# A decoder layer on one core: the expert weights' split moved from GpSimd to ScalarE and VectorE, and the causal mask moved from a matrix product to a GpSimd selection

## The chip, the cores and the metric

The kernel runs on one core of a Trainium2 chip. The metric is the device time of one execution in microseconds. A core has five engines with a queue of instructions each: TensorE (PE in the profile, its weight loads PEld), VectorE (DVE), ScalarE (ACT), GpSimd (POOL) and SyncE (SP), which here only issues DMAs. Every queue runs in order, and the queues wait for each other with semaphores.

## The reference, cut to what matters

```
x (16, 128, 256), ctx (16, 128, 64): 16 sequences of 128 tokens
1. self-attention, 16 heads of 16, one shared key and value head, causal:
     scores = where(key <= query, q k / 4, min);  weights = softmax(scores);  x = layernorm(x + out(weights v))
2. cross-attention on ctx, 32 query heads on 8 key heads of 8, no mask:  x = layernorm(x + xattn(x, ctx))
3. feed-forward: a base network (256 -> 2*512 -> 256, silu(gate)*up) for every token, and 8 experts of the
   same shape of which a token takes the best 2 of softmax(x @ gate_w):
     x = layernorm(x + base(x) + sum over the 2 of share * expert(x))
```

## The kernel before, in words

The work is two blocks one after the other.

**The attention block** is a software pipeline over the 16 sequences. Five lists, `PE_ORDER`, `ACT_ORDER`, `DVE_ORDER`, `POOL_ORDER` and `SP_ORDER`, give each engine its order of stages within one step; an entry is (stage, unit, delta), and in step s the stage works on sequence s + delta. The order is written out by hand, and every stage waits on semaphores for what it reads and for the buffer that it overwrites. `s_` stages belong to self-attention, `c_` stages to cross-attention, `x2_turn` turns the finished row block `stream` over for the second block. Fp32 operands of the big products are split in two (a high part in fp32r and the low remainder), and products are summed from three of the four combinations.

Stages that matter here: `s_max` makes masked scores with queries on the partitions, whose row maxima VectorE takes (L626, a reduction); the maxima go back into the operands (`s_shift`), and `s_main` makes the scores a second time with keys on the partitions. In `s_main` each 512-column bank starts with a bf16 product of the identity with the mask `mask_kq` (L845) and then adds the scores (L846). `s_exp` (ScalarE, L493) takes the exponential into `prob`, `s_sum` (PE, L857) multiplies it with the values, with a column of ones for the denominators. For the layer norms VectorE runs a small chain `newton` of one-column operations (L711, L714, L717) and then `s_ln` (L729) or `c_ln` (L771), which scale a 128x256 tile; in `DVE_ORDER` both L717 and then L729 stand ahead of the maxima of `s_max`.

Beside this, the block splits the experts' weights. For each of 16 halves of expert weights (`HALF` = 1536 columns), SP loads `raw_w` (L359), GpSimd copies the high part (`w_high`, L401) and subtracts for the low part in three pieces (`w_low`, L406), and SP stores both parts to DRAM (`store_w`, L363). Other GpSimd stages are `s_split` (L390, low part of x), `c_keys` (L435, two products), `x_bias` (L426) and, twice in all, `base_split` (L415, L417).

**The experts block** starts behind a barrier. PE computes the router's logits for all tokens (L1432, 32 products that the profile counts as 64), VectorE and ScalarE turn them into choices, the positions of the chosen tokens are found, and 39 sorted tiles of 128 tokens run through the chosen experts while the base network fills in before and after. GpSimd gathers the rows of tile j + 3 (L1107) and scatters the results of tile j (L1113), both as indirect DMAs. The split weights of an expert come back in one 3 MB load (L1067) into one of three slots; the layout in DRAM is `(EXPERTS, P, 2, 2, HALF)`, one piece of 24 KB for each partition. For a sorted tile, PE reads two registers out of SBUF and waits for the weights with one of them:

```
slot_of[j] = pe.value_load(tile_slot[0:1, j:j + 1], min_val=0, max_val=RING - 1)
needed = pe.value_load(tile_ready[0:1, j:j + 1], min_val=1, max_val=EXPERTS)
free_inner(u, h)
if h == 0:
    pe.wait_ge(sem["weights_ready"], needed)
```

Of the kernel before, what the change touches and what calls it, by code (L numbers as in the profile page):

```python
# [7 lines left out]
F32 = mybir.dt.float32  # L8
# [10 lines left out]
P = 128  # L19
# [6 lines left out]
CONST_COLS = 3 * P + 22  # L26
# [13 lines left out]
HT_RING = 5  # L40
ROUTE_COLS = 2 * P + SLOTS + EXPERTS * EXPERTS + PICKS + 1 + EXPERTS
# [16 lines left out]
    ("x2_turn", 0, -2),  # L58
# [13 lines left out]
    ("c_ln", 0, -2), ("c_rows", 0, 1), ("c_den", 0, -1), ("c_den", 1, -1), ("c_out", 0, -1), ("c_out", 1, -1),  # L72
    ("s_max", 1, 3), ("c_res", 0, -1), ("s_den", 0, 2), ("c_stats", 0, -1), ("s_out", 0, 2), ("c_max", 0, 1), ("s_bias", 0, 4),
# [3 lines left out]
    ("s_split", 0, 4), ("w_high", 0, 2), ("c_keys", 0, 1), ("w_low", 0, 2), ("w_low", 1, 2),  # L77
    ("x_bias", 0, 2), ("w_low", 2, 2), ("base_split", 0, 2),
# [3 lines left out]
    ("store_w", 0, 1), ("load_w", 0, 3), ("store_x2", 0, -2),  # L82
# [24 lines left out]
    "x2_turn": [("x2_read", 1, 1)],  # L107
}
# [81 lines left out]
def decoder_layer(nc, x, xT, ctx, ctxT, wqkvT, bqkv, woT, bo, gate_w, base_gu, base_down, expert_w, consts, routing, out):  # L190
    x2 = nc.dram_tensor("x2", (B * S, D), F32, kind="Internal").ap()
    shared = nc.dram_tensor("chosen_y", (CHOICES * B * S, D), F32, kind="Internal").ap()
    split = nc.dram_tensor("split_w", (EXPERTS, P, 2, 2, HALF), F32, kind="Internal").ap()
    with ExitStack() as both:
        def sb(name, shape, dt=F32, scope=both):
# [10 lines left out]
        gate = sb("gate", [P, 2, EXPERTS])  # L206
        base_loaded = both.enter_context(nc.semaphore("base_loaded"))
# [4 lines left out]
                  gate_w, gate, base_hi, base_lo, base_dn, base_loaded, base_split, expert_w, split, split_stored, xT2, x2, x2_stored)  # L212
        experts(nc, split, split_stored, routing, x2, x2_stored, shared, stream, xT2, ident, eps, gate, base_hi, base_lo, base_dn,
# [3 lines left out]
def attention(nc, x, xT, ctx, ctxT, wqkvT, bqkv, woT, bo, consts, stream, ident, eps, base_gu, base_down,  # L217
              gate_w, gate, base_hi, base_lo, base_dn, base_loaded, base_split, expert_w, split, split_stored, xT2, x2, x2_stored):
    score_ring, prob_ring, sum_ring, misc_ring = rings()
    with ExitStack() as scope:  # L220
# [3 lines left out]
        def two(name, shape, dt=F32):  # L224
# [10 lines left out]
        mask_qk, mask_kq = sb("mask_qk", [P, 4, P], BF16), sb("mask_kq", [P, 4, P], BF16)  # L235
        blk_s, blk_c = cst[:, 3 * P:3 * P + 2], cst[:, 3 * P + 2:3 * P + 6]
        neg_s, neg_c = cst[0:32, 3 * P + 6:3 * P + 14], cst[0:32, 3 * P + 14:3 * P + 22]
# [46 lines left out]
        names = """w_high w_low x2_turned x2_read base_high consts_loaded weights_loaded w_hi w_split wo_split tables values_set  # L284
            xT_hi_set xT_split x_biased s_qkv_full s_qkv_read s_rows_hi s_rows_lo s_q_full s_q_read s_k_full s_k_read
            s_max_full s_max_read s_shift_full s_shift_read s_main_full s_exp s_summed s_sum_read
            s_out_full s_den_set s_ctx s_ctx_full s_ctx_hi s_ctx_read s_res_full s_res_read s_stats s_mv s_ln s_rsqrt0
# [33 lines left out]
        def _(sp):  # L321
# [49 lines left out]
            for p in range(2):  # L371
                sp.wait_ge(split_stored[p], 16 * EXPERTS)

        @block.gpsimd
        def _(pool):

            for p in range(2):
                pool.memset(v_s[p][:], 0.0)
                zero = pool.memset(v_c[p][:], 0.0)
# [15 lines left out]
            def w_high(seq, unit):  # L395

                p = seq.odd
                wait_loaded(pool, w_loaded, seq)
                if seq.off >= 2:
                    wait_loaded(pool, split_stored, seq.back(2))  # L400
                pool.tensor_copy(halves[p][:, 0, :], raw_w[p][:]).then_inc(sem["w_high"], 1)  # L401

# [547 lines left out]
def experts(nc, split, split_stored, routing, x2, x2_stored, shared, stream, xT2, ident, eps, gate, base_hi, base_lo, base_dn,  # L950
            base_loaded, base_split, out):
    with ExitStack() as scope:
# [147 lines left out]
        def _(pool):  # L1100
# [16 lines left out]
            for j in range(AHEAD):  # L1117
                gather(j)
# [539 lines left out]
```

## Time and profile before

| what | value |
|---|---|
| median of 3 runs | 762.73 us (762.64 to 770.33) |
| the profiled execution's own time | 764.03 us |
| its span | 762.2 us |
| PE busy | 632.4 us, 83% |
| DVE busy | 476.9 us, 63% |
| ACT busy | 307.3 us, 40% |
| POOL busy | 224.8 us, 29% |

The profile is of one execution. Busy time is a sum over both blocks: the attention block ends at about 411 us, the sorted tiles run from 473 to 704 us, and the rest is the base network and the last layer norm. An engine counts as busy also while its instruction is held up inside.

### The profile page before, as it was taken

The page shows a single profiled execution, that of the slowest core. Times are in us where ns is not written, and L with a number is a line of the kernel's source. Part 1 is how long each engine was busy: PE and PEld are TensorE (multiplying, and loading weights), DVE is VectorE, ACT ScalarE, POOL GpSimd, SP SyncE. Part 2 cuts the span into 40 slices and gives each one's busy share as a digit, 9 for nine tenths or more (in the row PEclk, how much of TensorE's full clock was granted, in tenths as well). Part 3 has the DMA queues.
Part 4 walks back from the last instruction along what each step waited for, and adds up shares of the span by engine and source line. Part 5 has one row for each costly group of instructions (what it writes and reads, how often), then busy time and mean ns, then how long its engine had stood idle before and what let it go on. Part 6 is the DMA issues. An engine that isn't in the chain of part 4 may idle for free. (4 is left out here: it accounts for less than half of the span.)

```text
span 762.2 us, 11308 instructions
## 1 busy us (share of the span) xinstructions
PE 632.4 (83%) x3379; PEld 436.6 (57%) x3379; DVE 476.9 (63%) x972; ACT 307.3 (40%) x657; POOL 224.8 (29%) x223
## 2 busy tenths in 40 slices
PE   3767989898898898899767998997898888998981
PEld 2444435555454545454335876776686776777770
DVE  4578998988888988978762472333333333344286
ACT  2435656655656655565553211222222222223114
POOL 2344653244432244423200002233333333332100
PEclk9989999999999999999997799999999999999997
DMA  8241344413444313342204800015515542110513
GB/s 265 84 152 59 138 138 153 150 65 105 152 139 153 130 65 124 138 145 105 90 14 149 374 0 28 29 53 197 210 42 201 208 152 92 44 47 24 183 39 110
DMA packets 34727, 90.46 MB, mean 119 GB/s; under 512 B 6028, under 2 KB 24975, under 8 KB 33648
## 3 DMA queue, kind: packets, MB, share of 16 engines
q1 hardware_dynamic: 30928, 80.43, 29.5%
q0 software_dynamic: 3744, 9.31, 3.8%
q8 instruction: 32, 0.52, 0.3%
q14 instruction: 23, 0.19, 0.1%
HBM read 56.18 MB, written 34.47 MB: 119 GB/s over the span
## 5 line engine op out<-in xcount | busy, mean ns | idle before, releaser
L1135 ACT ACTIVATE silu<-inner 128x512 f32<-128x512 f32 x55 | 32.9, 598 | 185.4 <-PE inner L1523 135.1
L493 ACT ACTIVATE prob<-scores 128x1024 f32<-128x1024 f32 x96 | 98.2, 1025 | 13.1 <-PE scores L846 7.8
L1296 DVE TENSOR_TENSOR hT<-hiddenT,hT 128x512 fp32r<-128x512 f32 x39 | 27.0, 692 | 111.5 <-ACT hT L1141 111.5
L1113 POOL DMA_INDIRECT chosen_y<-y_rows,to_row x39 | 40.0, 1026 | 161.2 <-DVE y_rows L1311 161.2
L1518 PE MATMUL inner<-weights,sT_hi 128*128 x156 | 69.1, 443 | 20.9 <-issue 20.9
L626 DVE TENSOR_REDUCE max_c<-scores 128x8 f32<-128x1024 f32 x64 | 77.9, 1217 | 5.8 <-PE scores L909 4.3
L919 PE MATMUL scores<-q_c,k_c 128*128 128x512 f32 x128 | 48.0, 458 | 33.3 <-DVE max_s L626 26.9
L390 POOL TENSOR_TENSOR xT_lo<-xT_in,xT_hi 128x256 fp32r<-128x256 f32 x16 | 11.9, 747 | 192.5 <-ACT xT_hi L464 192.5
L1107 POOL DMA_INDIRECT rows<-x,from_row x39 | 38.1, 978 | 91.9 <-DVE from_row L1278 80.4
L933 PE MATMUL sums<-prob,v_c 128*32 128x512 f32 x256 | 63.0, 604 | 0.0
L1519 PE MATMUL inner<-weights,sT_hi 128*128 x156 | 61.8, 396 | 0.0
L406 POOL TENSOR_TENSOR halves<-raw_w,halves 128x512 fp32r<-128x512 f32 x48 | 60.9, 1283 | 0.1
L919 PEld LDWEIGHTS scores<-q_c,k_c 128*128 128x128 f32 x128 | 20.4, 201 | 60.2 <-issue 54.3
L1523 PE MATMUL inner<-weights,sT_lo 128*128 x156 | 49.0, 395 | 0.0
L909 PE MATMUL scores<-k_c,q_c 96*128 96x512 f32 x128 | 45.7, 438 | 3.9 <-DVE max_c L626 3.9
L626 DVE TENSOR_REDUCE max_s<-scores 128x8 f32<-128x1024 f32 x32 | 38.9, 1217 | 14.7 <-PE scores L822 14.6
L1518 PEld LDWEIGHTS inner<-weights,sT_hi 128*128 128x128 f32 x156 | 29.6, 190 | 31.1 <-issue 28.1
L435 POOL TENSOR_TENSOR k_c<-k_split,cst 96x512 fp32r<-96x512 f32 x32 | 32.7, 1043 | 38.8 <-DVE k_split L735 38.8
L1553 PE MATMUL y<-weights,hT 128*128 x156 | 42.7, 305 | 0.5 <-ACT hT L1141 0.4
L822 PE MATMUL scores<-k_s,q_s 96*128 96x256 f32 x128 | 39.8, 427 | 0.0
L1554 PE MATMUL y<-weights,hT 128*128 x156 | 39.7, 286 | 0.0
L857 PE MATMUL sums<-prob,v_s 128*64 128x512 f32 x128 | 34.5, 618 | 0.0
(217 smaller groups left out, 1482.1 us busy)
## 6 DMA issues: line engine op xcount, KB each, us to landing
split_w<-halves SPq DMA_DIRECT2D x16, 1536.0 KB, 6.6
weights<-split_w SPq DMA_DIRECT2D x8, 3072.0 KB, 11.2
raw_w<-in_expert_w SPq DMA_DIRECT2D x16, 768.0 KB, 8.1
weights<-chosen_y SPq DMA_DIRECT2D x8, 512.0 KB, 7.4
xT_in<-in_xT SPq DMA_DIRECT2D x16, 128.0 KB, 2.7
x_in<-in_x SPq DMA_DIRECT2D x16, 128.0 KB, 2.4
x<-stream SPq DMA_DIRECT2D x16, 128.0 KB, 1.7
ctxT_in<-in_ctxT SPq DMA_DIRECT2D x16, 96.0 KB, 2.3
```

The costliest lines, as they stand in the source:

```text
L406: pool.tensor_tensor(halves[p][:, 1, n * third:n * third + n], raw_w[p][:, n * third:n * third + n], f32(halves[p][:, 0, n * third:n * thi ...
L493: act.activation(prob[:, m, :], scores[:, n, :], ACT.Exp, scale=scale).then_inc(sem[exped], 1)
L626: dve.tensor_reduce(out_[:, 8 * unit:8 * unit + 8], scores[:, n, :].rearrange("p (h k) -> p h k", k=S), AX.X, ALU.max).then_inc(sem[read], 1)
L822: mm = pe.matmul(scores[:, n, at + 256 * v:at + 256 * v + 256], q_s[p][0:96, 4 * unit + 2 * bank + v, :], k_s[p][0:96], start=False, stop= ...
L909: mm = pe.matmul(scores[:, n, 512 * v:512 * v + 512], q_c[p][0:96, 2 * unit + v, :], k_c[p][0:96, unit // 2], start=True, stop=True)
L919: mm = pe.matmul(scores[:, n, 512 * v:512 * v + 512], k_c[p][:, a, 2 * (unit % 2) + v, :], q_c[p][:, 4 * a:4 * a + 4, :], start=True, stop ...
L933: mm = pe.matmul(sums[32 * j:32 * j + 32, n, :], v_c[p][:, a, 32 * j:32 * j + 32], prob[:, m, 512 * v:512 * v + 512], start=True, stop=True)
L1113: pool.indirect_dma_start(out=shared, out_offset=bass.IndirectOffsetOnAxis(ap=to_row[:, j:j + 1], axis=0), in_=y_rows[j % 3][:], in_offset ...
L1518: pe.matmul(into, sT_hi[j % 2][:, k, :], w(0, k), start=(k == 0), stop=False)
L1519: pe.matmul(into, sT_hi[j % 2][:, k, :], w(1, k), start=False, stop=False)
L1523: mm = pe.matmul(into, sT_lo[j % 2][:, k, :], w(0, k), start=False, stop=(k == 1))
L1553: pe.matmul(into, hT[:, j % 2, 0, P * c:P * c + P], w(0, c), start=(c == 0), stop=False)
```

## The change

- `mask_kq` and its product in `s_main` go. Between `s_exp` and `s_sum` stands a new GpSimd stage `s_causal`, which sets the weights of later keys to zero in place, by index; `s_sum` waits for it in place of `s_exp`.
- `w_high` moves to ScalarE, in two halves of 768 columns; `w_low` moves to VectorE, in three pieces of 512 columns, one step later. `store_w` comes one step earlier relative to its input. `base_split` comes two steps earlier.
- The split weights lie in DRAM in pieces of 512 columns (2 KB); a half's high and low part are stored by two DMAs, and the load of an expert moves 12 pieces for each partition.
- The logits are computed in the attention block, sequence by sequence (`x2_logit` on PE, then ScalarE copies them to SBUF). The experts block starts without those products.
- The wait for an expert's weights moves from PE to GpSimd: a new `go(j)` reads `tile_ready`, waits and increments a semaphore `go` on which PE waits with a constant. PE keeps the other register.
- An expert's padded count is at least 128; `y_rows` shares memory with `lane_hot`.

```diff
-CONST_COLS = 3 * P + 22
+CONST_COLS = 2 * P + 22
+PIECE = 512
+PIECES = HALF // PIECE
 PE_ORDER = [
...
-    ("x2_turn", 0, -2),
+    ("x2_logit", 0, -3), ("x2_turn", 0, -2),
 ]
 ACT_ORDER = [
...
-    ("s_rsqrt", 0, 1), ("c_read", 1, -1), ("c_rows", 0, 1), ("c_exp", 0, 0), ("s_read", 0, 2),
-    ("c_exp", 1, 0), ("c_turn", 0, 1), ("c_exp", 2, 0), ("c_values", 0, 1), ("s_read", 1, 2),
-    ("c_exp", 3, 0), ("s_rows", 0, 4), ("x2_read", 0, -2),
+    ("s_rsqrt", 0, 1), ("w_high", 0, 2), ("c_read", 1, -1), ("c_rows", 0, 1), ("c_exp", 0, 0), ("s_read", 0, 2),
+    ("c_exp", 1, 0), ("c_turn", 0, 1), ("c_exp", 2, 0), ("c_values", 0, 1), ("w_high", 1, 2), ("s_read", 1, 2),
+    ("c_exp", 3, 0), ("s_rows", 0, 4), ("x2_logit", 0, -3), ("x2_read", 0, -2),
 ]
 DVE_ORDER = [
...
-    ("c_ln", 0, -2), ("c_rows", 0, 1), ("c_den", 0, -1), ("c_den", 1, -1), ("c_out", 0, -1), ("c_out", 1, -1),
-    ("s_max", 1, 3), ("c_res", 0, -1), ("s_den", 0, 2), ("c_stats", 0, -1), ("s_out", 0, 2), ("c_max", 0, 1), ("s_bias", 0, 4),
+    ("c_ln", 0, -2), ("w_low", 0, 1), ("c_rows", 0, 1), ("w_low", 1, 1), ("c_den", 0, -1), ("c_den", 1, -1), ("c_out", 0, -1), ("c_out", 1, -1),
+    ("s_max", 1, 3), ("c_res", 0, -1), ("s_den", 0, 2), ("c_stats", 0, -1), ("s_out", 0, 2), ("c_max", 0, 1), ("s_bias", 0, 4), ("w_low", 2, 1),
     ("s_shift", 0, 3),
 ]
 POOL_ORDER = [
-    ("s_split", 0, 4), ("w_high", 0, 2), ("c_keys", 0, 1), ("w_low", 0, 2), ("w_low", 1, 2),
-    ("x_bias", 0, 2), ("w_low", 2, 2), ("base_split", 0, 2),
+    ("s_causal", 0, 2), ("s_split", 0, 4), ("c_keys", 0, 1), ("s_causal", 1, 2), ("x_bias", 0, 2), ("base_split", 0, 2),
 ]
 SP_ORDER = [
     ("load_xT", 0, 4), ("load_ctx", 0, 2), ("load_base", 0, 2), ("load_x", 0, 2),
-    ("store_w", 0, 1), ("load_w", 0, 3), ("store_x2", 0, -2),
+    ("store_w", 0, 0), ("load_w", 0, 3), ("store_x2", 0, -2),
 ]
...
-    split = nc.dram_tensor("split_w", (EXPERTS, P, 2, 2, HALF), F32, kind="Internal").ap()
+    split = nc.dram_tensor("split_w", (EXPERTS, 4 * PIECES, P, PIECE), F32, kind="Internal").ap()
...
             def store_w(seq, unit):
                 wait(sp, sem["w_low"], seq, 3)
-                sp.dma_start(split[seq.off // 2, :, :, seq.odd, :], f32(halves[seq.odd][:])).then_inc(split_stored[seq.odd], 16)
+                for part in range(2):
+                    at = PIECES * (2 * part + seq.odd)
+                    sp.dma_start(split[seq.off // 2, at:at + PIECES].rearrange("c p n -> p c n"),
+                                 f32(halves[seq.odd][:, part, :]).rearrange("p (c n) -> p c n", n=PIECE)).then_inc(split_stored[seq.odd], 16)
...
+            def s_causal(seq, b):
+
+                m = prob_ring.slot("s_exp", b, seq)
+                wait(pool, sem["s_exp"], seq, 2, b + 1)
+                keys_first = prob[:, m, :].rearrange("p (h q) -> p h q", q=S)
+                pool.affine_select(keys_first, keys_first, [[0, 8], [1, S]], ALU.is_ge, no_weight, base=0, channel_multiplier=-1)\
+                    .then_inc(sem["s_causal"], 1)
...
+            def w_high(seq, unit):
+
+                p, n = seq.odd, HALF // 2
+                wait_loaded(act, w_loaded, seq)
+                if unit == 0 and seq.off >= 2:
+                    wait_loaded(act, split_stored, seq.back(2), 2)
+                act.copy(halves[p][:, 0, n * unit:n * unit + n], raw_w[p][:, n * unit:n * unit + n]).then_inc(sem["w_high"], 1)
+
+            def x2_logit(seq, unit):
+                n = misc_ring.slot("x2_logit", 0, seq)
+                wait(act, sem["x2_logit"], seq)
+                act.copy(logits[:, seq.off, :], misc[:, n, 0:EXPERTS]).then_inc(sem["x2_logit_read"], 1)
...
+            def w_low(seq, third):
+                p, n = seq.odd, HALF // 3
+                if third == 0:
+                    wait(dve, sem["w_high"], seq, 2)
+                dve.tensor_tensor(halves[p][:, 1, n * third:n * third + n], raw_w[p][:, n * third:n * third + n],
+                                  f32(halves[p][:, 0, n * third:n * third + n]), ALU.subtract).then_inc(sem["w_low"], 1)
...
                 for bank in range(2):
                     at = 512 * bank
-                    pe.matmul(scores[:, n, at:at + 512], ident_b[:], mask_kq[:], start=True, stop=False)
                     mm = pe.matmul(scores[:, n, at:at + 512], k_s[p][:, b, :], q_s[p][:, 4 * bank:4 * bank + 4, :],
-                                   start=False, stop=True)
+                                   start=True, stop=True)
...
-                wait(pe, sem["s_exp"], seq, 2, b + 1)
+                wait(pe, sem["s_causal"], seq, 2, b + 1)
...
+            def x2_logit(seq, unit):
+                n = misc_ring.slot("x2_logit", 0, seq)
+                wait(pe, sem["x2_read"], seq)
+                if seq.off == 0:
+                    pe.wait_ge(base_loaded, 48)
+                misc_ring.wait_free(pe, sem, "x2_logit", 0, seq)
+                for k in range(2):
+                    mm = pe.matmul(misc[:, n, 0:EXPERTS], xT2[:, k, S * seq.off:S * seq.off + S], gate[:, k, :], start=(k == 0), stop=(k == 1))
+                mm.then_inc(sem["x2_logit"], 1)
...
-                sp.dma_start(f32(weights[:, e % RING]), split[e]).then_inc(weights_loaded[e], 16)
+                sp.dma_start(f32(weights[:, e % RING]).rearrange("p a k (c n) -> p (a k c) n", n=PIECE), split[e].rearrange("c p n -> p c n")).then_inc(weights_loaded[e], 16)
...
+            def go(j):
+
+                if j == 0:
+                    pool.wait_ge(sem["tile_set"], 1)
+                needed = pool.value_load(tile_ready[0:1, j:j + 1], min_val=1, max_val=EXPERTS)
+                pool.wait_ge(sem["weights_ready"], needed)
+                pool.sem_inc(sem["go"], 1)
 
             for j in range(AHEAD):
                 gather(j)
+            go(0)
+            go(1)
             for j in range(SORTED):
                 if j + AHEAD < SORTED:
                     gather(j + AHEAD)
+                if j + 2 < SORTED:
+                    go(j + 2)
                 scatter(j)
...
-            for t in range(B):
-                for k in range(2):
-                    mm = pe.matmul(logits[:, t, :], xT2[:, k, P * t:P * t + P], gate[:, k, :], start=(k == 0), stop=(k == 1))
-            mm.then_inc(sem["logits_full"], 1)
...
-                    needed = pe.value_load(tile_ready[0:1, j:j + 1], min_val=1, max_val=EXPERTS)
+                    pe.wait_ge(sem["go"], j + 1)
                 free_inner(u, h)
-                if h == 0:
-                    pe.wait_ge(sem["weights_ready"], needed)
```

## Rows read from the trace of the kernel before

**Rows 1.** Busy time by stretch: start:end, length, engines' busy us (instructions), PE clock, DMA

```profile
200.00:300.00 100.00, 88.44 (x471) 49.27 (x470) 87.30 (x171) 59.22 (x133) 41.29 (x39) 0.97 0.34 116
412.00:419.00 7.00, 7.00 (x34) 7.00 (x34) 1.39 (x4) 0.81 (x1) 0.00 (x0) 0.50 0.95 346
530.00:704.00 174.00, 151.75 (x869) 126.76 (x870) 62.52 (x115) 43.47 (x88) 56.01 (x56) 0.99 0.31 112
```

**Rows 2.** Groups by shape, DVE: busy us, mean ns of one, idle before

```profile
L717 DVE SCALAR_TENSOR_TENSOR t_s<-t_s,r_s 128x1 f32<-128x1 f32 x16 | 25.9, 1622 | 0.1
L729 DVE TENSOR_SCALAR x<-pre,mv_s,t_s 128x256 f32<-128x256 f32 x16 | 17.3, 1079 | 0.1
L717 DVE SCALAR_TENSOR_TENSOR t_c<-t_c,r_c 128x1 f32<-128x1 f32 x16 | 15.3, 954 | 0.1
```

**Rows 3.** DVE in order of time, from four steps: start us, us

```profile
179.70 1.79 DVE L717 SCALAR_TENSOR_TENSOR t_s<-t_s,r_s 128x1 f32<-128x1 f32 x1
...
182.64 0.88 DVE L729 TENSOR_SCALAR x<-pre,mv_s,t_s 128x256 f32<-128x256 f32 x1
183.44 1.21 DVE L626 TENSOR_REDUCE max_s<-scores 128x8 f32<-128x1024 f32 x1
...
202.10 1.79 DVE L717 SCALAR_TENSOR_TENSOR t_s<-t_s,r_s 128x1 f32<-128x1 f32 x1
...
321.30 2.07 DVE L729 TENSOR_SCALAR x<-pre,mv_s,t_s 128x256 f32<-128x256 f32 x1
...
382.42 0.15 DVE L717 SCALAR_TENSOR_TENSOR t_s<-t_s,r_s 128x1 f32<-128x1 f32 x1
```

**Rows 4.** POOL in order of time, one step

```profile
178.18 2.03 POOL L435 TENSOR_TENSOR k_c<-k_split,cst 96x512 fp32r<-96x512 f32 x2
180.18 2.50 POOL L406 TENSOR_TENSOR halves<-raw_w,halves 128x512 fp32r<-128x512 f32 x2
182.65 0.71 POOL L426 TENSOR_TENSOR x_bias<-x_in,b_o 128x256 f32<-128x256 f32 x1
```

**Rows 5.** Groups by shape that price the new and removed operations

```profile
L417 POOL TENSOR_TENSOR base_lo<-raw_base,base_hi 128x1024 fp32r<-128x1024 f32 x2 | 4.8, 2401 | 0.2
L415 POOL CAST base_hi<-raw_base 128x1024 fp32r<-128x1024 f32 x2 | 2.2, 1103 | 0.0
L845 PE MATMUL scores<-mask_kq,ident_b 128*128 128x512 bf16 x64 | 24.9, 389 | 3.0 <-DVE q_s L639 1.5 <-ACT prob L493 1.2 <-DVE max_c L626 0.3
```

**Rows 6.** ACT in order of time: idle before in brackets

```profile
180.84 0.59 ACT L512 COPY sumT_c<-sums 128x512 f32<-128x512 f32 x1 [1.68 <-PE sums L933]
...
196.90 1.03 ACT L493 ACTIVATE prob<-scores 128x1024 f32<-128x1024 f32 x1
...
221.71 0.40 ACT L464 CAST xT_hi<-xT_in 128x256 fp32r<-128x256 f32 x1
```

**Rows 7.** PE in order of time, the long wait of a step

```profile
207.20 0.70 PE L919 MATMUL scores<-q_c,k_c 128*128 128x512 f32 x2 [1.90 <-DVE max_s L626]
```

**Rows 8.** The start of the experts block, in order of time

```profile
411.95 13.79 PE L1432 MATMUL route<-gate,xT 128*128 128x8 f32 x64 [1.16 <-PEq L220]
...
414.77 1.22 DVE L1201 TENSOR_TENSOR xg_lo<-xT,xg_hi 128x1024 fp32r<-128x1024 f32 x1
...
425.78 0.29 DVE L1206 TENSOR_REDUCE stat_max<-route 128x16 f32<-128x128 f32 x1 [9.79 <-PE route L1432]
```

**Rows 9.** Who waited for whom: us in total, times, longest us

```profile
PE inner L1518 <- issue: 20.9, 36, 0.8
PE turned L1539 <- DMA rows<-x,from_row: 10.5, 6, 2.4
```

**Rows 10.** The chain that ended last, its longest piece: start us, us

```profile
518.19 9.19 DMA rows<-x,from_row
```

**Rows 11.** DMA issues: KB each, median us to landing

```profile
weights<-split_w SPq DMA_DIRECT2D x8, 3072.0 KB, 11.2
...
xT_in<-in_xT SPq DMA_DIRECT2D x16, 128.0 KB, 2.7
```

More of the change, by code:

```diff
@@ L206, in decoder_layer @@
         gate = sb("gate", [P, 2, EXPERTS])
+        logits = sb("logits", [P, B, EXPERTS])
         base_loaded = both.enter_context(nc.semaphore("base_loaded"))
@@ L393, in s_split @@
                     pool.tensor_tensor(wo_lo[:], raw_wo[:], f32(wo_hi[:]), ALU.subtract).then_inc(sem["wo_split"], 1)
[L395 to L401, printed above, removed]
-            def w_low(seq, third):
-                p, n = seq.odd, HALF // 3
-                wait(pool, sem["w_high"], seq)
-                pool.tensor_tensor(halves[p][:, 1, n * third:n * third + n], raw_w[p][:, n * third:n * third + n],
-                                   f32(halves[p][:, 0, n * third:n * third + n]), ALU.subtract).then_inc(sem["w_low"], 1)
+            def s_causal(seq, b):
[4 more added lines that the diff above has]
+                    .then_inc(sem["s_causal"], 1)
             def split_base(seq, unit):
-                k = seq.off - 3
+                k = seq.off - 1
                 if k == 0:
@@ L438, in c_keys @@
                 ins.then_inc(sem["ctx_k_set"], 1)
-            run(pool, POOL_ORDER, dict(s_split=s_split, x_bias=bias, c_keys=c_keys, w_high=w_high, w_low=w_low,
-                                       base_split=split_base))
+            run(pool, POOL_ORDER, dict(s_causal=s_causal, s_split=s_split, x_bias=bias, c_keys=c_keys, base_split=split_base))
         @block.scalar
@@ L576, in _ @@
                                      s_proj=s_proj, s_log=s_log, s_rsqrt=s_rsqrt, c_keys=c_keys, c_values=c_values, c_rows=c_rows,
-                                     c_turn=c_turn, c_exp=c_exp, c_read=c_read, c_log=c_log, c_rsqrt=c_rsqrt, x2_read=x2_read))
+                                     c_turn=c_turn, c_exp=c_exp, c_read=c_read, c_log=c_log, c_rsqrt=c_rsqrt, x2_read=x2_read, w_high=w_high, x2_logit=x2_logit))
         @block.vector
@@ L947, in _, with experts @@
                          s_proj=s_proj, s_res=s_res, c_turn=c_turn, c_max=c_max, c_shift=c_shift, c_main=c_main,
-                         c_sum=c_sum, c_out=c_out, x2_turn=x2_turn))
-def experts(nc, split, split_stored, routing, x2, x2_stored, shared, stream, xT2, ident, eps, gate, base_hi, base_lo, base_dn,
+                         c_sum=c_sum, c_out=c_out, x2_turn=x2_turn, x2_logit=x2_logit))
+def experts(nc, split, split_stored, routing, x2, x2_stored, shared, stream, xT2, eps, ident, logits, base_hi, base_lo, base_dn,
             base_loaded, base_split, out):
@@ L1004, in experts @@
         hidden = [lane_hot[:, 8 * p:8 * p + 8, :].rearrange("p a b -> p (a b)").bitcast(F32) for p in range(2)]
+        y_rows = [lane_hot[:, 16 + 4 * p:20 + 4 * p, :].rearrange("p a b -> p (a b)").bitcast(F32) for p in range(3)]
         slot_hot = sb("slot_hot", [P, PICKS, SLOTS], BF16)
@@ L1204, in shift_logits @@
             def shift_logits():
-                dve.wait_ge(sem["logits_full"], 1)
-                then(dve.tensor_reduce(stat["max"][:], logits, AX.X, ALU.max))
-                then(dve.tensor_tensor(gates["shifted"][:], logits, each(stat["max"][:]), ALU.subtract))
+                then(dve.tensor_reduce(stat["max"][:], logits[:], AX.X, ALU.max))
+                then(dve.tensor_tensor(gates["shifted"][:], logits[:], each(stat["max"][:]), ALU.subtract))
             def choose_first():
```

38 lines of the change are left out of this document (19 added, 19 removed).

## The prediction

> **What bounds the kernel now.** I read the busy time by stretch first, since the two blocks have different limits [rows 1]. In a steady stretch of attention PE is busy 88% and DVE 87% of the time, ACT 59%: two engines share the limit. In the sorted tiles PE is busy 87% and DVE 36%: PE alone is the limit. At the start of the experts block the granted clock of PE is 0.50, that is 1.2 GHz of 2.4.
>
> Then the groups by shape. A DVE operation of one column, L717, takes 1622 and 954 ns in the mean, though the last step's took 0.15 us [rows 2, 3]; L729 takes 1079 ns in the mean and 0.41 us in the last step, where GpSimd was idle. Laid beside GpSimd's own instructions the ends agree: L717 of 179.70 ends at 181.49, the first of GpSimd's two L406, which take 2.50 us from 180.18, at about 181.43; L729 ends at 183.52, `x_bias` L426 at 183.36 [rows 3, 4]. So these three VectorE operations run only when a GpSimd instruction ends. Then comes the reduction L626, and PE has idled 1.90 us for it [rows 7]. That is the binding chain of a step, and a step is 202.10 - 179.70 = 22.4 us.
>
> The excess is L717: 25.9 + 15.3 - 32 x 0.15 = 36.4 us, and L729: 17.3 - 16 x 0.41 = 10.7 us: 47 us in all [rows 2]. In the step shown it is 1.64 us for the first L717, about 1.15 for the second, which ends where L729 starts, and 0.47 for L729: 3.26 us. In some steps L729 loses a second time, to the last L406, as at 321.30 with 2.07 us, which adds 1.2 us [rows 3]; I take this for 5 steps of 13. The mean is then about 3.7 us, and 47 / 3.7 says that some 13 steps pay it in full.
>
> **Attention, what GpSimd frees and what it takes on.** Removed from GpSimd are the copy and the three subtractions; added are two selections of 128x1024 for a step. Their price X is in no row. The nearest rows are a one-input copy of 1024 columns, 1.10 us, and a two-input operation of 1024 columns, 2.40 us [rows 5]. A selection reads one tensor, as the copy does, but makes indices; I take 1.5 us, nearer to the copy, and keep 1.1 and 2.4.
>
> When is GpSimd done in the new order? `s_exp` of unit 0 ends at 197.93, which is 175.5 one step earlier [rows 6]. From there: selection X, `s_split` 0.7, `c_keys` 2.0, selection X, `x_bias` 0.7 [rows 4] (`s_split` is of the size of `x_bias`), with the instructions' small overlaps and the second exponential, which ends at 178.7, already over: 179.0 + 2X, so 182.0. If DVE waits for all of it, L729 ends at 182.4 and the reduction starts then, not at 183.44: 1.0 us a step. The second loss to a last L406 cannot happen any more: 0.5 us in the mean. Together 1.5 x 13 = 19.5 us. `s_sum` of unit 0 stands on PE right ahead of the idle 1.90 us that end at 207.20 [rows 7] and takes 1.1 us, so it ran at 204.2, or 181.8 one step earlier; its selection would end at 177.0: not a new wait.
>
> Costs in the same step. (a) Three `w_low` on DVE, 512 columns each; 1024 columns with both inputs in SBUF took 1.22 us [rows 8], so 0.65 each, 1.95 a step. DVE idles 12.7% of a step, 2.8 us [rows 1]. By the order lists I put 1.2 us of this between the two `s_max` reductions, where DVE waits for PE and where the first two stand, and 0.3 us ahead of `s_shift`, where the third stands. Left over: 0.2 + 0.35 us. (b) Two `w_high` on ACT of 768 columns, 0.59 us for 512 scaled to 0.85, placed before `c_read` 1, which has 1.68 us of idle ahead of it [rows 6], and before `s_read` 1 in a similar hole (ACT is idle 41% of a step, 9 us [rows 1]): nothing, as long as their data is there; without that cover 0.85 us each. (c) On PE the masks leave: 4 products a step, of 389 ns but pipelined, and a mask and its scores together follow the next pair in 0.46 us, so half of that each: -0.9 us [rows 5]; the logits come: 4 records at 13.79 / 64 = 0.22 us at the halved clock [rows 8], +0.5 to +0.9. PE is not last where either stands, so I count -0.2 for the masks and +0.25 for the logits and their copy on ACT ahead of `s_proj`. Costs 0.6 x 13 = 8 us. Attention in all: -12 us. With X = 1.1 it is 0.8 less a step, -22; with X = 2.4 it is 1.8 more, +11.
>
> The rule behind this chain stands in the Trainium skill, SBUF — State Buffer, section Who interferes with whom: a DVE instruction with two SBUF inputs contends with a GpSimd instruction that reads SBUF, and the holder keeps the port for the whole instruction. By that rule the moved `w_low`, two inputs in SBUF, could itself be held; the rows put it at 184.9, after GpSimd's 182.0, so it changes nothing here unless X is over 2.9. For X the skill (GPSIMD Engine Reference, section Elementwise — side-by-side cycle accounting) states 1.8 cycles an element for a tight loop at 1.2 GHz: an estimate of 1.54 us for 1024, and the sum would be 1 us higher.
>
> **SP's queue.** `load_w` now waits for `w_low` 2 late in DVE's step, and `store_x2`, the next `load_xT`, `load_ctx`, `load_x` and `store_w` are queued behind it. I put its issue at 215.3 and that of xT at 216.4; xT landed 2.7 us after issue in the median before [rows 11], now behind 768 KB of weights, so at 220 to 220.7; ACT needs it at 221.71 [rows 6]. About 1 us of slack: no cost counted.
>
> **Between the blocks.** The 13.79 us of logits leave the path [rows 8]. What is late next: VectorE's `xg_lo`, which ends at 415.99 because it stands behind the load of the routing constants [rows 8]; the routing chain then starts at 416.0 and not at 425.78: -9.8 us. The attention block ends later by one logit product and its copy, +1.0. If PE starts its base products at full clock up to 2 us more may come. Taken: -9 us.
>
> **The sorted tiles, register and weights wait.** PE idles 20.9 us in 36 places ahead of the first product of a tile, 0.58 each, put down to issue [rows 9]: that is two register reads and two waits. One read and the wait on a register leave. Bounds 0 (if the reads overlap) and 20.9; no row separates them, so I take half, -10 us. On GpSimd `go(j+2)` stands behind the gather and ahead of the scatter of j; the rows of a tile (5.7 us long) leave about 1.3 us before PE would wait for it, and a `go` costs at most what PE's pair of reads does. Nothing counted.
>
> **The sorted tiles, the gathers.** In 6 places PE idles for a gather, 10.5 us in all; the gather of 518.19 took 9.19 us [rows 9, 10]. It is the first of five such pieces in the chain, one for each of the five later weight loads of 3 MB, which take 11.2 us themselves and whose pieces are 24 KB for each partition [rows 11]. With 2 KB pieces the gather's packets have less to wait for. Bounds: 0 and -10.5; I take -7.
>
> Speaking against it is the Trainium skill, DMA: Bandwidth & Descriptors, section Queues, rings and completion order: an engine changes queues only after a packet of some 9 to 17 descriptors. Twelve pieces of 2 KB would then be as long as one of 24 KB, and this gain would be 0. No run here shows which.
>
> **The sum.** Against the profiled execution's own time: 764.0 - 12 - 9 - 10 - 7 = 726.0; that execution is 1.3 us over the median of the runs, so 724.7, say 725.
>
> **Rivals.**
> A. The port comes free (the selections do not hold it, or DVE wins between them): the 3.7 us go, and PE becomes the limit at 22.4 - 1.9 - 0.2, some 20.3 us a step. 2.7 x 13 = 35 in place of 12: 702. For it: in the last steps the three operations are short. Against: every other GpSimd instruction that reads SBUF held them.
> B. The sorted tiles keep their pace, since gathers wait as now and the register read was hidden: 725 + 17 = 742. For it: one read stays, and the gathers' start may depend on the load's bandwidth and not on its pieces.
> C. xT comes late through SP's queue and ACT waits about 1 us every step, with `c_read` and the second exponential behind it: 725 + 13 = 738.
> D. The slower side: the selection is slow. GpSimd's program for an index test may cost more than a two-input operation. Each further us of X costs 2 us a step, since DVE's chain waits for both selections. The gain elsewhere (26 us) and 2X against 2 x 1.5 break even at 13 x 2 x (X - 1.5) = 38, X = 2.95 us. With X = 4 the time is 725 + 65 = 790.
>
> Chances: the forecast 0.50, A 0.13, B 0.17, C 0.08, D 0.12. A measurement of this kernel tells about 1% from no change (755 to 770). The forecast's own range with X from 1.1 to 2.4 is 708 to 748. A reaches 702, X = 2.4 with B passes 752 a little; I give 700 to 752, which leaves out D and the edges. Faster by over 1%: 0.84; within 1%: 0.06; slower: 0.10.
>
> **What would show it.** The selection's mean ns; L717 and L729 means near 0.7 to 1.0 us and not 1.6; a step near 21.4 us; idle of PE before L919 gone or smaller; the L1518 issue idle near 0.3 us; gathers landing in 4 us during weight loads; the routing chain starting about 4.5 us after the barrier. Wrong would make it: GpSimd longer in a step than before, ACT waiting for `raw_w` or xT, or PE waiting for `go`.

## The result, and the profile after

The changed kernel takes 707.8 us (median of 4 runs, 706.6 to 711.0) where the kernel before takes 766.5 in the same rounds: a ratio of 0.924, 95% interval 0.916 to 0.932. The profiled execution took 708.4 us with a span of 706.3; before it was 764.0 and 762.2. The forecast was 725, its range 700 to 752. One run of experiment 4 below (723.9 us) fell in a slower state of the chip and is left out.

Four marks in the traces split the span into stages, in this and every later kernel: VectorE's first computation into `t_s` (there is one for each sequence, and a step of attention runs from one to the next), VectorE's first instruction of the experts block (`ones_b`), TensorE's first product of the first sorted tile, and its first product of the second half of the last one.

| | before | after | difference |
|---|---|---|---|
| attention ends at | 411.9 | 393.1 | -18.8 |
| mean of 11 steps, from the first mark behind 80 us | 23.4 | 20.8 | -2.5 |
| from there to the first sorted tile | 61.4 | 51.9 | -9.5 |
| first to last sorted tile | 227.0 | 199.1 | -27.9 |
| behind it | 61.9 | 62.3 | +0.4 |

Busy time by stretch of the kernel after, with the columns of [rows 1]:

```profile
200.00:300.00 100.00, 96.11 (x520) 53.78 (x525) 93.02 (x203) 74.11 (x165) 27.71 (x30) 1.00 0.42 145
470.00:640.00 170.00, 164.79 (x969) 139.30 (x968) 68.91 (x128) 47.82 (x99) 64.15 (x65) 1.00 0.42 141
```

TensorE went from 88% to 96% in a stretch of attention, and from 87% to 97% in the sorted tiles. VectorE is at 93% in the same stretch of attention, its time behind GpSimd included, but TensorE no longer waits for its maxima. TensorE's longest waits in 200:300, before and after:

```profile
PE scores L919 <- DVE max_s L626: 9.5, 5, 1.9
...
PE misc L831 <- ACT q_s L488: 2.2, 5, 0.5
PE misc L919 <- DVE ctx_c L780: 1.2, 4, 0.3
```

TensorE itself is the limit now, in a step of attention and in the tiles. Its granted clock rose too, from 0.97 to 1.00 of 2.4 GHz in 200:300. An estimate from these two figures: 0.03 of a step of 23.4 us is 0.7 us, so that the clock can hold up to that much of the 2.5 us by which a step is shorter. No run parts it from the waits that went.

The groups of VectorE that answer to [rows 2], and GpSimd's selection:

```profile
L731 DVE SCALAR_TENSOR_TENSOR t_s<-t_s,r_s 128x1 f32<-128x1 f32 x16 | 14.5, 904 | 0.1
L743 DVE TENSOR_SCALAR x<-pre,mv_s,t_s 128x256 f32<-128x256 f32 x16 | 11.7, 731 | 0.1
L731 DVE SCALAR_TENSOR_TENSOR t_c<-t_c,r_c 128x1 f32<-128x1 f32 x16 | 2.4, 149 | 0.1
...
L409 POOL TENSOR_SCALAR_AFFINE_SELECT prob<-prob 128x1024 f32<-128x1024 f32 x32 | 34.9, 1092 | 229.2 <-ACT prob L495 229.2
```

One step of the kernel after in order of time, VectorE and then GpSimd (answers to [rows 3, 4]):

```profile
212.41 0.91 DVE L731 SCALAR_TENSOR_TENSOR t_s<-t_s,r_s 128x1 f32<-128x1 f32 x1
213.25 0.15 DVE L731 SCALAR_TENSOR_TENSOR t_c<-t_c,r_c 128x1 f32<-128x1 f32 x1
213.36 0.81 DVE L743 TENSOR_SCALAR x<-pre,mv_s,t_s 128x256 f32<-128x256 f32 x1
214.09 1.21 DVE L640 TENSOR_REDUCE max_s<-scores 128x8 f32<-128x1024 f32 x1
...
212.21 1.10 POOL L409 TENSOR_SCALAR_AFFINE_SELECT prob<-prob 128x1024 f32<-128x1024 f32 x1
213.27 0.74 POOL L429 TENSOR_TENSOR x_bias<-x_in,b_o 128x256 f32<-128x256 f32 x1
```

The first operation still ends with a GpSimd instruction (213.32 and 213.31), and `x` with the next one; what they lose is 0.76 and 0.40 us, not the 3.26 us of before. The waits of TensorE in the tiles, and the chain's gathers ([rows 9, 10] before):

```profile
PE turned L1573 <- DMA rows<-x,from_row: 7.1, 6, 2.3
PE inner L1552 <- issue: 0.2, 1, 0.2
```

```profile
485.79 6.56 DMA rows<-x,from_row
```

The 20.9 us of issue idle are gone entirely, not by half. The gathers behind a weight load take 6.3 to 7.3 us where they took 8.1 to 9.2, and six places still wait. One of the six, of 2.4 and 2.3 us, stands ahead of the first sorted tile; inside the tiles the waits are 8.1 us in five places before, and 4.8 after.

The start of the routing chain, for [rows 8]:

```profile
393.06 0.17 DVE L1396 MEMSET ones_b<- 128x128 bf16 x1 [2.79 <-PEq L225]
...
396.80 0.28 DVE L1246 TENSOR_REDUCE stat_max<-logits 128x16 f32<-128x128 f32 x1
```

It starts 3.7 us into the block; before it was 13.9 (411.86 to 425.78).

### The profile page after: what moved, and what is told of

Read it like the earlier page. It is cut to its first block and busy times, and to the rows that moved or that the text cites. A ratio compares the mean times of both kernels' runs of the same rounds, so it can differ in the third digit from the quotient of the medians.

```text
span 706.3 us, 11300 instructions
## 1 busy us (share of the span) xinstructions
PE 620.5 (88%) x3300; PEld 427.0 (60%) x3315; DVE 473.5 (67%) x1019; ACT 334.8 (47%) x705; POOL 176.6 (25%) x191
## 5 line engine op out<-in xcount | busy, mean ns | idle before, releaser
L409 POOL TENSOR_SCALAR_AFFINE_SELECT prob<-prob 128x1024 f32<-128x1024 f32 x32 | 34.9, 1092 | 229.2 <-ACT prob L495 229.2
L1142 POOL DMA_INDIRECT chosen_y<-lane_hot,to_row x39 | 40.0, 1026 | 134.3 <-DVE lane_hot L1351 131.0
L953 PE MATMUL sums<-prob,v_c 128*32 128x512 f32 x256 | 65.9, 635 | 0.0
L1553 PE MATMUL inner<-weights,sT_hi 128*128 x156 | 61.5, 394 | 0.0
L939 PE MATMUL scores<-q_c,k_c 128*128 128x512 f32 x128 | 46.3, 443 | 8.8 <-DVE q_c L653 4.0
L764 DVE TENSOR_TENSOR halves<-raw_w,halves 128x512 fp32r<-128x512 f32 x48 | 37.0, 770 | 0.0
L843 PE MATMUL scores<-k_s,q_s 96*128 96x256 f32 x128 | 36.4, 398 | 0.0
L1188 ACT CAST sT_hi<-turned 128x256 fp32r<-128x256 f32 x39 | 14.6, 374 | 46.0 <-PE turned L1573 46.0
## 6 DMA issues: line engine op xcount, KB each, us to landing
weights<-split_w SPq DMA_DIRECT2D x8, 3072.0 KB, 13.1
```

Source lines behind the costliest of these rows:

```text
L939: mm = pe.matmul(scores[:, n, 512 * v:512 * v + 512], k_c[p][:, a, 2 * (unit % 2) + v, :], q_c[p][:, 4 * a:4 * a + 4, :], start=True, stop ...
L953: mm = pe.matmul(sums[32 * j:32 * j + 32, n, :], v_c[p][:, a, 32 * j:32 * j + 32], prob[:, m, 512 * v:512 * v + 512], start=True, stop=True)
L1142: pool.indirect_dma_start(out=shared, out_offset=bass.IndirectOffsetOnAxis(ap=to_row[:, j:j + 1], axis=0), in_=y_rows[j % 3], in_offset=No ...
L1553: pe.matmul(into, sT_hi[j % 2][:, k, :], w(1, k), start=False, stop=False)
```

## Experiments

These are twelve kernels, each with four runs, but 5 and 6 with two. They ran on several chips, so that two kernels are best compared by their ratios. Ratios are against the kernel before in the same rounds; "steps", "attention", "first tile" and "tiles" are the marks above, from each kernel's trace.

| kernel | us | ratio (95%) | steps | attention | first tile | tiles |
|---|---|---|---|---|---|---|
| before | 766.5 | | 23.4 | 411.9 | 473.3 | 227.0 |
| after | 707.8 | 0.916-0.932 | 20.8 | 393.1 | 445.0 | 199.1 |
| 1 before + split moved | 727.5 | 0.942-0.953 | 20.5 | 375.8 | 436.9 | 226.2 |
| 2 before + selection | 801.8 | 1.039-1.049 | 25.5 | 454.3 | 516.0 | 222.8 |
| 3 after, masks on TensorE | 706.7 | 0.914-0.925 | 21.1 | 394.2 | 446.1 | 197.8 |
| 4 after, selections twice | 717.2 | 0.931-0.943 | 21.7 | 398.6 | 450.2 | 197.5 |
| 5 before + `go` | 755.7 | 0.978-0.989 | 23.4 | 415.0 | 476.2 | 215.2 |
| 6 after + a register read | 725.2 | 0.939-0.950 | 20.8 | 392.2 | 444.1 | 217.8 |
| 7 after, 24 KB pieces | 718.1 | 0.929-0.939 | 20.8 | 391.9 | 443.5 | 210.3 |
| 8 after, gathers 5 ahead | 700.1 | 0.905-0.917 | 20.8 | 392.0 | 441.7 | 192.0 |
| 9 best | 694.1 | 0.895-0.910 | 20.5 | 377.2 | 438.7 | 190.9 |
| 10 best, 24 KB pieces | 694.5 | 0.894-0.909 | 20.5 | 377.9 | 439.3 | 191.3 |
| 11 best, selections | 698.1 | 0.899-0.915 | 20.3 | 380.6 | 442.2 | 191.0 |
| 12 best, logits in the steps | 696.2 | 0.903-0.918 | 21.1 | 390.3 | 438.9 | 191.1 |

**1. The kernel before with the split moved** off GpSimd, with the order lists of the kernel after (no selections, no logits in them).

```diff
-    ("s_split", 0, 4), ("w_high", 0, 2), ("c_keys", 0, 1), ("w_low", 0, 2), ("w_low", 1, 2),
-    ("x_bias", 0, 2), ("w_low", 2, 2), ("base_split", 0, 2),
+    ("s_split", 0, 4), ("c_keys", 0, 1), ("x_bias", 0, 2), ("base_split", 0, 2),
     (w_high on ScalarE, w_low on VectorE)
```

> The kernel before, with the splitting of the weights moved to ScalarE and VectorE (with the order lists of the kernel after) and nothing else: masks stay on TensorE, the router's logits stay in the experts block, the waits and pieces are as before. Theory 1 (freeing GpSimd's port is the gain): the one-column operations fall from 1622 ns to under 0.9 us, the step falls to where TensorE with its masks limits it, about 22 us; attention ends near 400 to 406, 752 to 760 in all. Theory 2 (VectorE and ScalarE pay for the split what the port gave): no change or up to 10 us slower, 763 to 775.

Attention alone takes 36 us less, more than the whole change brings there, and a step takes 20.5 us, shorter than that of the kernel after. Theory 1 was right in kind and far too small in size. VectorE, one step and its groups:

```profile
185.94 0.16 DVE L710 SCALAR_TENSOR_TENSOR t_s<-t_s,r_s 128x1 f32<-128x1 f32 x1
186.06 0.16 DVE L710 SCALAR_TENSOR_TENSOR t_c<-t_c,r_c 128x1 f32<-128x1 f32 x1
186.14 0.41 DVE L722 TENSOR_SCALAR x<-pre,mv_s,t_s 128x256 f32<-128x256 f32 x1
186.47 1.22 DVE L619 TENSOR_REDUCE max_s<-scores 128x8 f32<-128x1024 f32 x1
```

```profile
L743 DVE TENSOR_TENSOR halves<-raw_w,halves 128x512 fp32r<-128x512 f32 x48 | 35.0, 729 | 0.0
...
L710 DVE SCALAR_TENSOR_TENSOR t_s<-t_s,r_s 128x1 f32<-128x1 f32 x16 | 3.0, 186 | 0.1
```

```profile
183.01 2.04 POOL L420 TENSOR_TENSOR k_c<-k_split,cst 96x512 fp32r<-96x512 f32 x2
185.01 0.73 POOL L411 TENSOR_TENSOR x_bias<-x_in,b_o 128x256 f32<-128x256 f32 x1
```

GpSimd is done at 185.74, before VectorE's three operations begin at 185.94. They take 0.16, 0.16 and 0.41 us; the first took 0.15 in the last step of the kernel before [rows 3]. The three `w_low` of a step, 2.2 us, cost nothing that shows: TensorE is 97.7% busy in 200:300, and no longer waits for `max_s` there.

**2. The kernel before with the selection alone**: masks off TensorE, two selections on GpSimd, the split still there.

```diff
-    pe.matmul(scores[...], ident_b[:], mask_kq[:], start=True, stop=False)
+    pool.affine_select(keys_first, keys_first, [[0, 8], [1, S]], ALU.is_ge, no_weight, ...)
```

> The kernel before, with the selection on GpSimd in place of the mask products; the weights are still split on GpSimd. Theory 1 (GpSimd's port sets the step before): GpSimd is 2.2 us longer in a step, VectorE's three operations run later; attention ends 5 to 30 us later than 411.8, 770 to 792 in all. Theory 2 (the masks on TensorE are what costs): attention ends 10 to 15 us sooner, 748 to 755.

Theory 1 holds, and past its bound: the kernel is 34 us slower, and attention ends 42 us later and not 5 to 30. With 2.2 us more of GpSimd a step is 2.1 us longer. Two things stand in that: TensorE's waits for `max_s` grow from 22.4 to 37.7 us in 84:341, and its granted clock in 200:300 is 0.91 and not 0.97. One step, GpSimd and VectorE:

```profile
216.84 2.05 POOL L444 TENSOR_TENSOR k_c<-k_split,cst 96x512 fp32r<-96x512 f32 x2
218.83 1.10 POOL L401 TENSOR_SCALAR_AFFINE_SELECT prob<-prob 128x1024 f32<-128x1024 f32 x1
219.89 2.49 POOL L415 TENSOR_TENSOR halves<-raw_w,halves 128x512 fp32r<-128x512 f32 x2
...
217.67 3.54 DVE L726 SCALAR_TENSOR_TENSOR t_s<-t_s,r_s 128x1 f32<-128x1 f32 x1
221.13 1.30 DVE L726 SCALAR_TENSOR_TENSOR t_c<-t_c,r_c 128x1 f32<-128x1 f32 x1
```

A one-column operation stood 3.54 us, from 217.67 to 221.21, past the ends of three GpSimd instructions (about 217.9, 218.9 and 219.9), and ended at that of the fourth.

**3. The kernel after with the masks back on TensorE** and no selection.

```diff
+    pe.matmul(scores[:, n, at:at + 512], ident_b[:], mask_kq[:], start=True, stop=False)
-    ("s_causal", 0, 2), ("s_split", 0, 4), ("c_keys", 0, 1), ("s_causal", 1, 2), ("x_bias", 0, 2), ...
+    ("s_split", 0, 4), ("c_keys", 0, 1), ("x_bias", 0, 2), ...
```

> The kernel after, with the causal mask of the self attention back in the score products on TensorE and no selection on GpSimd. Theory 1 (TensorE is the limit of a step now, 96% busy in 200:300): four mask products a step come back, 0.23 to 0.39 us each, so 0.9 to 1.5 us a step and 12 to 20 us in all; attention ends near 405 to 413 and not at 393, the whole takes 720 to 728. Theory 2 (the VectorE chain behind GpSimd's port still sets the step, as the prediction had it): GpSimd loses 2.2 us a step, VectorE starts sooner, the mask hides on TensorE; attention ends at 393 or sooner, 695 to 708 in all.

The total falls under theory 2, its reason does not: 706.7 against 707.8 is no difference, and attention ends 1 us later, not sooner. The step is 0.2 us longer with four mask products in it. That is a net figure. By the busy share in 200:300, TensorE works 97.3% of a step of 21.2 us here and 96.1% of 21.0 in the kernel after. That is 20.6 and 20.2 us, so that the masks cost it some 0.45 us, 0.11 each and not 0.23 to 0.39 (experiments 9 and 11 differ in the same way, 97.7% of 20.5 and 96.2% of 20.3); their records (389 ns each, [rows 5]) lie over those of the scores. The other 0.25 us came back as idle time: the 1.2 us in 200:300 in which TensorE waited for VectorE's `ctx_c` are gone. VectorE's three operations fell in the mean from 0.90, 0.15 and 0.73 us to 0.19, 0.16 and 0.50, and that bought no more than this, since TensorE is the limit:

```profile
200.00:300.00 100.00, 97.32 (x532) 53.27 (x537) 88.15 (x204) 72.95 (x163) 17.11 (x20) 1.00 0.42 145
```

**4. The kernel after with every selection done twice.** The second changes nothing of the values.

```diff
+    pool.affine_select(keys_first, ...).then_inc(sem["s_once"], 1)
+    wait(pool, sem["s_once"], seq, 2, b + 1)
     pool.affine_select(keys_first, ...).then_inc(sem["s_causal"], 1)
```

> The kernel after, with every selection on GpSimd done twice in a row (the second changes nothing), so that X is 2.2 us and not 1.09. The prediction's slope (2 us a step for each us of X, since VectorE waits for both selections): 13 x 2.2 = 28 us more, 736 in all, the two one-column operations L731 and L743 means up by about 1 us each. Rival (TensorE is the limit, the port has slack at X = 1.09): under 10 us more, 708 to 718, with most of VectorE's longer waits eaten by its idle time.

The rival holds, at the edge of its range; the trace is of the fastest run, 711.6 us. A step is 0.9 us longer for 1.09 us more of X, a slope of 0.8 and not 2. GpSimd and VectorE in one step:

```profile
218.09 1.09 POOL L409 TENSOR_SCALAR_AFFINE_SELECT prob<-prob 128x1024 f32<-128x1024 f32 x1
219.25 1.09 POOL L411 TENSOR_SCALAR_AFFINE_SELECT prob<-prob 128x1024 f32<-128x1024 f32 x1
220.31 0.73 POOL L431 TENSOR_TENSOR x_bias<-x_in,b_o 128x256 f32<-128x256 f32 x1
...
217.13 1.03 DVE L733 SCALAR_TENSOR_TENSOR t_s<-t_s,r_s 128x1 f32<-128x1 f32 x1
218.08 0.15 DVE L733 SCALAR_TENSOR_TENSOR t_c<-t_c,r_c 128x1 f32<-128x1 f32 x1
218.20 1.14 DVE L745 TENSOR_SCALAR x<-pre,mv_s,t_s 128x256 f32<-128x256 f32 x1
219.26 1.21 DVE L642 TENSOR_REDUCE max_s<-scores 128x8 f32<-128x1024 f32 x1
```

`t_s` ended and `t_c` ran at 218.1, between `c_keys` and the first selection, and `x` between the first and the second; the reduction started at 219.26, 1.8 us before GpSimd was done. VectorE doesn't wait for all of GpSimd's list.

**5. The kernel before with `go` on GpSimd** in place of one register read and the weights wait on TensorE.

```diff
-    needed = pe.value_load(tile_ready[0:1, j:j + 1], min_val=1, max_val=EXPERTS)
-    pe.wait_ge(sem["weights_ready"], needed)
+    pe.wait_ge(sem["go"], j + 1)
```

> The kernel before, with one part of the change alone: GpSimd waits for a tile's weights and its own register read, and TensorE waits for the semaphore go. The weight store keeps its 24 KB pieces. Measured by the time from the first tile's first product to the last tile's (226 to 227 us in kernels with the old wait). Theory 1 (the register read and the wait on a register's value are the whole of the 20.9 us): 206 us, the rows put down to issue ahead of the first product near 0. Theory 2 (the prediction's, one read of two stays, so half is left): 216. Theory 3 (the smaller pieces gave it): 227.

The tiles take 215.2 us, between theories 1 and 2, and for another reason than theory 2 gave. Its waits:

```profile
PE turned L1549 <- DMA rows<-x,from_row: 17.7, 6, 3.3
```

No issue idle is left at all, so theory 1 is right of the cause. But the same six gathers are waited for 17.7 us in place of 10.5: TensorE comes to them sooner. Of 20.9 us 7.2 came back as that wait. The other 1.9 stand with a lower granted clock, 0.94 in 510:590 and in 590:670 against 0.98 and 1.00 before.

**6. The kernel after with one register read more on TensorE.**

```diff
+    pe.value_load(tile_ready[0:1, j:j + 1], min_val=1, max_val=EXPERTS)
     pe.wait_ge(sem["go"], j + 1)
```

> The kernel after, with one register read more on TensorE for each tile (the value isn't used), right ahead of its wait for go. If the read itself costs TensorE its 0.5 us, the tiles take 198 + 0.5 x 38 = 217 us and issue idle ahead of the first product comes back at about 20 us. If the cost was the wait against a register's value, or the wait for weights behind it, they stay at 198 us.

The second read brings the whole cost back, 0.58 us for each tile, though the wait behind it is on a constant:

```profile
PE turned L1574 <- DMA rows<-x,from_row: 2.5, 2, 2.3
PE inner L1553 <- issue: 21.4, 37, 0.7
```

The first read, of the slot, is there in the kernel after as well, with 0.2 us of issue idle in all: what costs is two reads one behind the other, not a read as such. With both in place the 2 KB pieces bring the gather wait down to 2.5 us, 2.3 of them ahead of the first tile: the idle time of the reads is then enough cover.

**7. The kernel after with the old layout of the split weights.**

```diff
-    split = nc.dram_tensor("split_w", (EXPERTS, 4 * PIECES, P, PIECE), F32, ...)
+    split = nc.dram_tensor("split_w", (EXPERTS, P, 2, 2, HALF), F32, ...)
```

> The kernel after, with the split weights laid out as before: stores in 6 KB pieces and loads in 24 KB pieces for each partition. If the smaller pieces let the gathers through (9.2 us to 6.3 to 7.3 us in the two traces), the gathers of tiles behind a weight load land in about 9 us again, the idle time ahead of the turning products goes from 7.1 back to about 10.5 us, and the tiles take 201 to 203 us and not 198 to 199. If the gathers came sooner for another reason (their start against the load's), nothing changes. In attention the stores have a third of the packets to make, so xT may land sooner than 4.7 us; nothing waits for it, no change of the step.

The expectation was right in direction and too small: the tiles take 11.2 us more. Waits, and one gather of the chain:

```profile
PE turned L1571 <- DMA rows<-x,from_row: 14.4, 6, 3.2
```

```profile
584.22 8.98 DMA rows<-x,from_row
```

The five gathers behind a weight load take 7.9 to 9.0 us, and 6.3 to 7.3 in the kernel after: the layout is the one difference. Of the 11.2 us, 7.3 are added wait; the other 4 stand with the granted clock, which is 0.96 in both halves of 480:640 and 1.00 in the kernel after.

**8. The kernel after with the gathers five tiles ahead.**

```diff
-AHEAD = 3
+AHEAD = 5
```

> The kernel after, with the gathers started five tiles ahead and not three. A gather that takes 6 to 9 us behind a weight load then has two tiles more (10 us) to land. If the idle 7.1 us of TensorE ahead of the turning products are gathers that start too late: they go, 198.5 to about 191.5 us for the tiles, 701 in all. If they are gathers held by the load whenever they start (the queue is full of the load's packets), the same places stay: 198 us, 708.

The first reading holds: 192.0 us. The one wait for a gather that is left stands ahead of the first tile:

```profile
PE turned L1573 <- DMA rows<-x,from_row: 2.4, 1, 2.4
```

**9 to 11. Put together**: experiment 1 with `go`, the 2 KB pieces and the gathers five ahead; the same with 24 KB pieces; the same with selections.

> Put together from the parts that paid alone: the weights split on ScalarE and VectorE, the masks on TensorE, the logits in the experts block as before, go on GpSimd, 2 KB pieces, gathers five tiles ahead. By the sum of stages: attention ends at 375.8 and the first tile starts at 436.9 (as with the moved split), the tiles take 192 (as with five ahead), 62 behind them and 2 around the span: 693 us. If the stages are not independent (the stores with small pieces take longer in attention, or the clock is lower at the start of the tiles), 697 to 703.

> As the last one, with the old layout of the split weights: 6 KB and 24 KB pieces. If the piece matters only through gathers that start too late, five tiles ahead hide it and the time is the same, 693 us, tiles in 192. If large pieces hold TensorE's gathers or the scatters in another way, 3 to 10 us more, tiles in 195 to 202.

> As the first of these, with the masks off TensorE and two selections on GpSimd. The step is 20.5 us with the masks and no logits. Theory 1 (TensorE is the limit, a mask costs it 0.2 us a step as 21.2 against 21.0 showed): a step of 20.3 us, 690 us in all. Theory 2 (the selections hold VectorE, whose operations wait for the port 0.7 us a step again, and the probabilities of the self attention come 1.1 us later): 20.5 to 21 us, 693 to 700.

The first takes 694.1 us, 13.7 less than the kernel after (in other rounds and on another chip: by the ratios, 0.902 against 0.924). The stages add up. The piece size is worth nothing once gathers start five tiles ahead (694.5), though it was worth 11 us of the tiles at three ahead. The selections shorten the step to 20.3 us and yet cost 4 us in all: on the same chip all four runs (696.0 to 699.1) lie above all four with masks (693.6 to 695.1). The first mark behind 80 us stands at 88.5 and not 83.0, so the loss is in the first steps. In 30:90 TensorE waits 7.5 us for VectorE's `rows_c` and not 4.2, 2.0 for `max_s` and not 1.3, and its granted clock is 0.91 and not 0.94. What holds VectorE there stays open.

**12. The fourth corner**: as 9, with the logits in the steps.

> The fourth corner of a square of two choices, all with gathers five tiles ahead: masks on TensorE or selections, logits in the steps or in the experts block. This one has the masks on TensorE and the logits in the steps. From the three others (694 masks and late logits, 698 selections and late logits, 700 selections and logits in the steps). If the two choices are independent (a mask costs TensorE what it costs anywhere), 696. If the moved logits are what costs, because TensorE has no room in a step, they cost most where the masks are there too: the first tile starts at 443 to 446 and not at 438.7, 699 to 703.

It takes 696.2 us, as if the two choices were independent (on another chip than 9; its ratio is 0.910 against 0.902, and the intervals overlap). With the logits in the steps attention ends 13.1 us later (390.3 against 377.2): 7.2 us in the ten steps that hold their products, 0.7 each, 4.3 behind these, and 1.6 ahead of the first mark. The 1.6 are not the logits' products, the first of which runs at 137.9 us. The change shortens the way to the first tile by 12.8 us (48.7 against 61.5). Moving them brings no gain that shows.

## Why the prediction was right in direction and 17 us too slow

**Attention, forecast -12, measured -18.8.** The step that failed is "If DVE waits for all of it, L729 ends at 182.4 and the reduction starts then". I let VectorE wait until GpSimd's list was done, so that GpSimd's shorter list gained only 1.5 us a step. The runs show that each of the three operations waits only until it gets in between two GpSimd instructions, which with the selections was at the next end (experiment 4, and the kernel after). With the instructions of 1.28 and 1.47 us gone (the means of `w_low` and `w_high` on GpSimd), the wait fell under what TensorE leaves, and TensorE became the limit: rival A, whose 20.3 us a step is what experiments 1 and 11 measured (20.5 and 20.3). I gave it 0.13. Its price for attention, -35, is the -36 of experiment 1. The kernel after shows less because of what it adds: 17.3 us (393.1 against 375.8), where I had put 8. Experiments 9, 11 and 12 have most of it apart: the selections end attention 3.4 us later (380.6 against 377.2), the logits' move 13.1. So the forecast of attention is near by luck in part: a gain that was put 17 us too small stood against costs that were put 9 too small.

A second term was left out. [rows 1] had TensorE's granted clock at 0.97 in 200:300, and I priced nothing for it; it rose to 1.00, which by the estimate above is worth up to 0.7 us a step.

**X, taken 1.5, measured 1.09 us**, the copy's price [rows 5]. The Trainium skill (GPSIMD Engine Reference, section Elementwise — side-by-side cycle accounting) gave an estimate of 1.54 us by its 1.8 cycles; the trace disagrees. By my own working this alone was worth 10 us (-22 with X = 1.1), which would have come near the measured 18.8 with the wrong slope. From 1.09 to 2.2 us the slope was 0.8 us a step for each us of X, not 2. If it stays so further up, which no run shows, rival D's break-even of 2.95 us was too low as well.

**The costs, 0.6 us a step.** `w_low` and `w_high` cost nothing visible. The masks' going was worth the 0.2 us a step that I put, as the net of 0.45 us of products and 0.25 of idle time that the selections brought. The logits were mis-sized: 0.25 us a step and 1.0 at the end became 0.7 in each step that has them and 4.3 behind. Their products, 10.6 us busy in all in the kernel after, went into an engine that has no room. I hid their cost because "PE is not last where either stands"; that ended with the change itself.

**SP's queue, nothing.** Right: xT landed in 4.7 us and not 2.7, and ACT waited for it once in 200:300, for 0.3 us. Rival C did not come.

**Between the blocks, -9.** Measured -9.5.

**Register and weights wait, -10.** The step "no row separates them, so I take half" failed: of 20.9 us 0.2 are left. But the term isn't independent of the next: alone it gave 11.8 us (experiment 5), with small pieces 18.7 (217.8 to 199.1).

**Gathers, -7.** The tiles lost 11.2 us without the small pieces (experiment 7), of which 7.3 are wait: within the rows' bounds only if the clock is left out. Rival B fell. I had read a gain of 0 out of the Trainium skill (DMA: Bandwidth & Descriptors, section Queues, rings and completion order), which has an engine change queues after a packet of about 9 to 17 descriptors. That took twelve pieces of 2 KB to be as long a packet as one of 24 KB. The section counts a packet in descriptors and does not say this, so it gives no gain of 0. The piece size does count here: 7.9 to 9.0 us for a gather with the old pieces and 6.3 to 7.3 with the new, but not the 4 us that I named. That small pieces let packets through sooner is argued, not shown: the loads also became slower, 11.2 to 13.1 us.

Where the sum missed: 6.8 us in attention, 10.9 in the tiles.

**Slips in the working.** They leave the forecast as it is. With X = 1.1 the forecast is 725 - 10 = 715 by its own working; no term gives the 708 that I named as the lower end. X = 2.4 with rival B is 748 + 17 = 765, 13 us past the range and not a little. Rival A's 2.7 us a step doesn't follow from its 22.4 - 20.3 = 2.1.

## What to carry to other kernels

When a change takes a wait away, ask first which engine is the limit behind it, and price everything that the change adds there at full cost: here the early logits were added to an engine that had slack before and none after, and the selections held VectorE in the first steps. With gathers five ahead the change without these two takes 694 us, with them 700; these ran on different chips and the intervals of their ratios overlap, and on one chip the selections alone cost 4 us. Price two waits in one queue together: time freed ahead of a late transfer comes back as a wait for it, unless the transfer also starts sooner. Here, starting a transfer two tiles sooner was a change of one constant and made the new memory layout needless.

## What the runs showed of the hardware that I had not expected

- A selection by index of 128x1024 float32 on GpSimd takes 1.09 us, as a copy of that size (1.10), less than half of a two-input operation (2.40).
- VectorE's operation of one column can be held by more than one GpSimd instruction: 3.54 us past three ends (experiment 2), 1.79 us past one [rows 3, 4], but it got in at the next end in experiment 4. The Trainium skill (SBUF — State Buffer, section Who interferes with whom) has the loser blocked for the whole instruction of the other; the trace shows that this is not the longest wait. What decides who gets in stays open.
- A second register read on TensorE, right behind another, costs 0.58 us of its idle time for each tile; the first alone leaves 0.2 us in all 39 tiles.
- Longer waits of TensorE in the tiles went with a lower granted clock: five of 2.6 to 3.3 us with a mean of 0.94 of 2.4 GHz (experiment 5, 510:670), five of 2.1 to 3.2 with 0.96 (experiment 7, 480:640), five of at most 1.5 with 1.00 (the kernel after).
- A bf16 mask product of 512 columns ahead of a score product costs a step some 0.11 us by the busy time, where its own record is 389 ns long (experiment 3).
